# New unit orders, split weights in two steps, a halved down projection and another first root in a fused attention and FFN kernel

## What is computed

```python
x = L0_attn_x                                  # (4, 512, 256), fp32
xn = _layernorm(x, axis=-1)
s = _L0_attn_ref(xn, Wq, Wk, Wv, Wo)           # 16 heads of 16, causal softmax
g = _silu(_L0_ffn_ref(xn, wq_gate, s_gate, wq_up, s_up, wq_down, s_down))
x = x + s * g
```

## Time and profile before

| | us |
|---|---|
| median of 3 runs (285.98 to 288.08) | 287.1 |
| the profiled execution | 287.32 |
| its span | 285.6 |
| TensorE busy in the span | 272.3 |
| VectorE busy | 209.5 |
| ScalarE busy | 174.0 |
| GpSimd busy | 133.1 |

### The profile page before, as it was taken

How to read it: one execution, slowest core, us unless ns; L and a number is a source line. 1 busy time by engine, 2 the same in 40 slices (tenths; PEclk the granted TensorE clock), 3 DMA queues, 4 the chain that set the end, 5 groups by cost and what they waited for, 6 DMA issues and landing times.

```text
span 285.6 us, 5873 instructions
## 1 busy us (share of the span) xinstructions
PE 272.3 (95%) x2088; PEld 202.0 (71%) x2088; DVE 209.5 (73%) x722; ACT 174.0 (61%) x258; POOL 133.1 (47%) x235
## 2 busy tenths in 40 slices
...
GB/s 266 328 165 203 182 5 2 76 3 112 187 220 9 3 0 6 76 182 153 190 6 6 0 2 3 37 42 137 158 158 77 2 3 2 148 3 3 2 2 73
DMA packets 18005, 23.11 MB, mean 81 GB/s; under 512 B 2936, under 2 KB 11064, under 8 KB 17976
## 3 DMA queue, kind: packets, MB, share of 16 engines
...
...
## 4 chain that ended last, share of the span: by engine, by line
PE 73%; DVE 17%; issue 2%; POOL 2%; DMA 2%; SPq 2%; ACT 1%; ACTq 1%; DVEq 0%
PE ps L428 15%; PE ps L430 12%; PE ps L429 12%; PE ps L578 12%; DVE ps L1007 10%; PE ps L561 8%; PE ps L543 6%; PE ps L588 3%; DMA tailt<-in_su 2%; DVE mx L1007 2%; PE ps L597 1%; PE ps L472 1%; DVE cn L1018 1%; POOL kp L809 1%; DVE hid L986 1%
## 5 line engine op out<-in xcount | busy, mean ns | idle before, releaser
L1007 DVE CUSTOM_DVE_ANT_0 ps<-ps,maskt 128x512 f32<-128x512 f32 (+3 forms) x256 | 117.5, 523 | 16.2 <-PE ps L543 15.7
L854 POOL TENSOR_SCALAR_AFFINE_SELECT pt<-pt 128x256 f32<-128x256 f32 (+1 forms) x112 | 47.7, 442 | 88.2 <-ACT pt L781 87.2
L781 ACT ACTIVATE pt<-ps 128x1024 f32<-128x1024 f32 x80 | 79.4, 1025 | 9.9 <-PE ps L561 8.3
L830 POOL TENSOR_TENSOR hid<-hid 128x512 f32<-128x512 f32 x24 | 32.0, 1333 | 18.4 <-DVE hid L986 9.4
L578 PE MATMUL ps<-pt,vt 128*32 128x256 f32 (+3 forms) x528 | 39.2, 439 | 0.3 <-DVE mx L1007 0.2
L428 PE MATMUL ps<-xh,guh 128*128 128x512 f32 x88 | 37.8, 430 | 1.1 <-DVE xr L979 0.4
L1007 DVE DVE_READ_ACCUMULATOR2_ANT mx<- 128x1 f32 x256 | 36.0, 141 | 0.0
L543 PE MATMUL ps<-kp,qp 64*128 64x512 f32 (+3 forms) x256 | 32.9, 342 | 2.0 <-DVE mx L1007 1.8
L430 PE MATMUL ps<-xh,gul 128*128 128x512 f32 x88 | 34.6, 393 | 0.0
L429 PE MATMUL ps<-xl,guh 128*128 128x512 f32 x88 | 34.5, 392 | 0.0
L561 PE MATMUL ps<-qp,kp 64*128 64x512 f32 (+3 forms) x256 | 33.1, 344 | 0.2 <-DVE mx L1007 0.2
(11 more groups left out here) (121 smaller groups left out, 497.5 us busy)
## 6 DMA issues: line engine op xcount, KB each, us to landing
...
```

Source lines behind the costliest of these rows:

```text
L781: nc.scalar.activation(pair(b, s), ps[:, b0:b1 + 1:b1 - b0, :], ACT.Exp, scale=SCALE).then_inc(exp_done, 1)
L830: nc.gpsimd.tensor_tensor(a, a, hid[:, m % 2, 1, :], ALU.mult).then_inc(h_done, 1)
L854: mm = nc.gpsimd.affine_select(out=diag, in_=diag, compare_op=ALU.is_ge, fill=0.0, base=0, pattern=[[0, diag.shape[1]], [1, P]], channel_m ...
L1007: mm = nc.vector.tensor_tensor_reduce(part, part, maskt[:, T - wide:], -1.0, TOP, ALU.add, ALU.min, mg[:, e, a // 2, i:i + 1])
```

## The change

- `WARM` goes from 36 to 26 zero products, and the four `FILL` products go.
- `transpose_x` waits for each tile of `xn` by itself. All `qk` and `gu` units of row 0 use `first_split`: both high weights by `xh`, both high weights by `xl`, then both low weights by `xh`, each with a wait of its own, so low weights are needed last. `qk:0:0` takes bank 2, which nothing held.
- Each down unit is cut in two, `da` and `dn`, of 17 products each.
- The first root: VectorE writes the variance plus epsilon, ScalarE takes its square root (`sq:0:0`), VectorE takes the reciprocal and does one Newton step (`rt:0:0`), 4 instructions.
- All five lists are new. On ScalarE `xhi` comes before `ghi:0:1` and `whi:0:2`. On VectorE the moments of row 1 come before `wds` and `qlo:0:0`, `wdl` after the first maxima. On TensorE nine projections come before `m:0:0` instead of six. In the tail `oa:3:0` comes after `zt:3:3` and `oa:3:1` after `z2:3:1`.
- The set of units is otherwise the same, with the same sizes.

```diff
@@ constants @@
 NEWTON = 3
-WARM = 36
-FILL = 4
+WARM = 26
 TENSOR_ORDER = """
-t:0:0:0 t:0:1:1 qk:0:0:0 qk:0:1:1 qk:0:2:2 gu:0:0:0 gu:0:1:1 qk:0:3:2 m:0:0:01 m:0:1:34 m:0:2:56 gu:0:2:7 gu:0:3:2
-gu:0:4:0 gu:0:5:7 m:0:3:12 m:0:4:34 gu:0:6:0 gu:0:7:1 gu:0:8:2 m:0:5:01 m:0:6:34 c:0:0:5 gu:0:9:6 v:0:0:0 v:0:1:1
-s:0:0:56 s:0:1:23 m:0:7:07 gu:0:10:4 s:0:2:01 m:0:8:56 s:0:3:23 m:0:9:57 s:0:4:01 m:0:10:26 m:0:11:35 m:0:12:01
-m:0:13:47 c:0:1:2 pv:0:0:6 m:0:14:05 m:0:15:23 t:1:0:1 dn:0:0:6 t:1:1:0 dn:0:1:2 c:0:2:7 qk:1:0:0 zt:0:0:1 m:0:16:23
-s:0:5:45 s:0:6:67 qk:1:1:1 m:0:17:02 s:0:7:34 s:0:8:56 qk:1:2:7 s:0:9:23 m:0:18:04 m:0:19:15 qk:1:3:6 s:0:10:23
...
-z2:3:0:0 dn:3:0:7 s:3:15:01 pv:3:2:2 s:3:16:01 s:3:17:34 s:3:18:56 zt:3:2:2 oa:3:0:7 s:3:19:01 dn:3:1:2 pv:3:3:0
-pv:3:4:1 zt:3:3:0 oa:3:1:2 zt:3:4:1 z2:3:1:0 z2:3:2:1 o:3:0 o:3:1
+t:0:0:0 t:0:1:1 qk:0:0:2 qk:0:1:0 gu:0:0:1 qk:0:2:3 gu:0:1:4 gu:0:2:5 qk:0:3:6 gu:0:3:4 gu:0:4:7 m:0:0:05 m:0:1:16
+gu:0:5:2 gu:0:6:0 gu:0:7:3 gu:0:8:2 m:0:2:17 m:0:3:03 gu:0:9:4 gu:0:10:1 t:1:0:5 m:0:4:06 m:0:5:37 v:0:0:4 m:0:6:02
+v:0:1:1 m:0:7:36 m:0:8:47 t:1:1:0 da:0:0:1 c:0:0:2 da:0:1:3 dn:0:0 m:0:9:02 s:0:0:45 s:0:1:67 dn:0:1 s:0:2:45
+m:0:10:02 s:0:3:67 qk:1:0:1 m:0:11:02 s:0:4:45 c:0:1:3 gu:1:0:6 m:0:12:02 m:0:13:17 m:0:14:34 pv:0:0:5 s:0:5:01
+qk:1:1:2 s:0:6:01 s:0:7:34 zt:0:0:5 gu:1:1:6 s:0:8:01 m:0:15:27 m:0:16:34 c:0:2:5 gu:1:2:6 m:0:17:57 s:0:9:01
...
+s:3:14:23 zt:3:1:7 da:3:0:5 c:3:3:6 dn:3:0 pv:3:2:0 s:3:15:12 s:3:16:34 s:3:17:56 z2:3:0:0 da:3:1:7 s:3:18:12
+s:3:19:34 zt:3:2:5 dn:3:1 pv:3:3:0 pv:3:4:1 zt:3:3:0 oa:3:0:2 zt:3:4:1 z2:3:1:0 oa:3:1:3 z2:3:2:1 o:3:0 o:3:1
 SCALAR_ORDER = """
-init:0:0 whi:0:0 whi:0:1 whi:0:2 ghi:0:0 ghi:0:1 xhi:0:0 xhi:0:1 woh:0:0 qhi:0:0 pkah:0:0 pkal:0:0 qhi:0:1 qhi:0:2
-wdh:0:0 tanh:0:0 up:0:0 qhi:0:3 hhi:0:0 tanh:0:1 up:0:1 tanh:0:2 hhi:0:1 up:0:2 tanh:0:3 hhi:0:2 up:0:3 tanh:0:4
-ccp:0:0 hhi:0:3 up:0:4 vcp:0:0 hhi:0:4 vcp:0:1 exp:0:0 exp:0:1 tanh:0:5 exp:0:2 exp:0:3 exp:0:4 up:0:5 xn:1:0 xn:1:1
...
+init:0:0 sq:0:0 whi:0:0 whi:0:1 ghi:0:0 xhi:0:0 xhi:0:1 ghi:0:1 whi:0:2 qhi:0:0 pkah:0:0 qhi:0:1 woh:0:0 qhi:0:2
+tanh:0:0 up:0:0 pkal:0:0 tanh:0:1 qhi:0:3 xn:1:0 up:0:1 hhi:0:0 wdh:0:0 hhi:0:1 xn:1:1 tanh:0:2 up:0:2 tanh:0:3
+up:0:3 xn:1:2 xn:1:3 hhi:0:2 hhi:0:3 tanh:0:4 up:0:4 tanh:0:5 up:0:5 hhi:0:4 vcp:0:0 hhi:0:5 vcp:0:1 xhi:1:0 xhi:1:1
...
 VECTOR_ORDER = """
-init2:0:0 st:0:0 xn:0:0 wlo:0:0 xn:0:1 xn:0:2 xn:0:3 wlo:0:1 wlo:0:2 xlo:0:0 xlo:0:1 glo:0:0 glo:0:1 qlo:0:0 wds:0:0
-qlo:0:1 qlo:0:2 wol:0:0 gate:0:0 wdl:0:0 qlo:0:3 maxa:0:0 maxb:0:0 gate:0:1 maxa:0:1 maxb:0:1 maxa:0:2 gate:0:2
-maxb:0:2 maxa:0:3 maxb:0:3 maxa:0:4 gate:0:3 maxb:0:4 sh:0:0 bn:1:0 maxa:0:5 gate:0:4 maxb:0:5 bn:1:1 bn:1:2 bn:1:3
-mom:1:0 maxa:0:6 maxb:0:6 maxa:0:7 maxb:0:7 maxa:0:8 maxb:0:8 gate:0:5 maxa:0:9 maxb:0:9 sh:0:1 maxa:0:10 maxb:0:10
...
+init2:0:0 st:0:0 rt:0:0 xn:0:0 xn:0:1 xn:0:2 xn:0:3 wlo:0:0 wlo:0:1 xlo:0:0 xlo:0:1 glo:0:0 glo:0:1 bn:1:0 bn:1:1
+bn:1:2 bn:1:3 mom:1:0 wds:0:0 qlo:0:0 gate:0:0 qlo:0:1 qlo:0:2 gate:0:1 qlo:0:3 wol:0:0 maxa:0:0 maxb:0:0 wdl:0:0
+gate:0:2 maxa:0:1 gate:0:3 maxb:0:1 wlo:0:2 maxa:0:2 maxb:0:2 maxa:0:3 maxb:0:3 gate:0:4 maxa:0:4 gate:0:5 maxb:0:4
+maxa:0:5 maxb:0:5 maxa:0:6 hlt:0:0 sh:0:0 maxb:0:6 maxa:0:7 xlo:1:0 maxb:0:7 maxa:0:8 maxb:0:8 bn:2:0 xlo:1:1 bn:2:1
...
 GPSIMD_ORDER = """
-init3:0:0 vones:0:0 sc:0:0 rows:0:3 rows:0:4 rows:0:5 hid:0:0 hlo:0:0 hid:0:1 hlo:0:1 hid:0:2 hlo:0:2 hid:0:3
...
+init3:0:0 rows:0:3 vones:0:0 rows:0:4 rows:0:5 sc:0:0 root:1:0 root:1:1 root:1:2 root:1:3 hid:0:0 hid:0:1 hlo:0:0
...
 SYNC_ORDER = """
-init4:0:0 loadx:1:0 pkh:0:0 pkl:0:0 pkh:0:1 pkh:0:2 pkh:0:3 pkl:0:1 pkl:0:2 pkl:0:3 loadres:0:0 crow:0:0 crow:0:1
-loadx:2:0 crow:0:2 pkh:1:0 pkl:1:0 pkh:1:1 pkl:1:1 pkh:1:2 pkh:1:3 crow:0:3 loadx:3:0 pkl:1:2 pkl:1:3 crow:1:0
...
+init4:0:0 loadx:1:0 pkh:0:0 pkh:0:1 pkh:0:2 pkl:0:0 pkl:0:1 pkh:0:3 pkl:0:2 pkl:0:3 loadres:0:0 loadx:2:0 crow:0:0
+pkh:1:0 crow:0:1 pkl:1:0 loadx:3:0 pkh:1:1 pkl:1:1 crow:0:2 pkh:1:2 pkl:1:2 crow:0:3 pkh:1:3 pkl:1:3 crow:1:0
...
...
                             w.need("gate", gate_done, HT * b + n // 2 + 1)
                         if n % 2 or n == GUN - 1:
                             w.need("up", up_done, HT * b + n // 2 + 1)
-                    elif kind == "dn":
+                    elif kind == "da":
                         w.need("u", u_done, KD * b + n + 1)
                     elif kind == "c":
                         w.need("ct", ct_copied, NG * b + n + 1)
@@ -466,27 +465,31 @@
 
             def transpose_x(b, k):
                 bank, = take(("t", b, k))
-                if k == 0:
-                    w.need("xn", xn_done, TT * (b + 1))
                 for i in range(TT):
+                    w.need("xn", xn_done, TT * b + i + 1)
                     mm = nc.tensor.transpose(ps[:, bank, i * P:(i + 1) * P], xn[:, i, k * P:(k + 1) * P], ident[:])
                 mm.then_inc(xt_ready, 1)
 
+            def first_split(dst, hi, lo, cols, hi_name, hi_sem, lo_name, lo_sem, part):
+
+                w.need(hi_name, hi_sem, part)
+                for k in range(KD):
+                    w.need("xhi", xhi_done, k + 1)
+                    nc.tensor.matmul(dst, hi[:, k, cols], xh[:, k, :], start=k == 0, stop=False)
+                for k in range(KD):
+                    w.need("xlo", xlo_done, k + 1)
+                    nc.tensor.matmul(dst, hi[:, k, cols], xl[:, k, :], start=False, stop=False)
+                w.need(lo_name, lo_sem, part)
+                for k in range(KD):
+                    mm = nc.tensor.matmul(dst, lo[:, k, cols], xh[:, k, :], start=False, stop=k == KD - 1)
+                return mm
+
             def project_qk(b, c):
                 bank, = take(("qk", b, c))
-                w.need("wl", wl_done, 1 if c == 0 else 2)
                 col = c * P
-                if b == 0 and c == 0:
-                    zeros(FILL, bank)
-                    for k in range(KD):
-                        w.need("xhi", xhi_done, k + 1)
-                        nc.tensor.matmul(ps[:, bank, :], wh[:, k, col:col + P], xh[:, k, :], start=k == 0, stop=False)
-                        nc.tensor.matmul(ps[:, bank, :], wl[:, k, col:col + P], xh[:, k, :], start=False, stop=False)
-                    for k in range(KD):
-                        w.need("xlo", xlo_done, k + 1)
-                        mm = nc.tensor.matmul(ps[:, bank, :], wh[:, k, col:col + P], xl[:, k, :], start=False,
-                                              stop=k == KD - 1)
-                    mm.then_inc(qk_ready, 1)
+                if b == 0:
+                    first_split(ps[:, bank, :], wh, wl, slice(col, col + P), "wh", wh_done, "wl", wl_done, min(c, 1) + 1
+                                ).then_inc(qk_ready, 1)
                     return
                 w.need("xlo", xlo_done, KD * (b + 1))
                 for k in range(KD):
...
 
             def gate_up(b, n):
                 bank, = take(("gu", b, n))
-                w.need("xlo", xlo_done, KD * (b + 1))
-                w.need("gul", gul_done, 1 if n % 2 == 0 else 2)
                 at = (n // 2 if n % 2 == 0 else HF + 1 + n // 2) * P
                 cols = slice(at, at + P)
+                if b == 0:
+                    first_split(ps[:, bank, :], guh, gul, cols, "guh", guh_done, "gul", gul_done, n % 2 + 1
+                                ).then_inc(gu_ready, 1)
+                    return
+                w.need("xlo", xlo_done, KD * (b + 1))
                 for k in range(KD):
                     mm = split3(ps[:, bank, :], guh[:, k, cols], gul[:, k, cols],
                                 xh[:, k, :], xl[:, k, :], k == 0, k == KD - 1)
                 mm.then_inc(gu_ready, 1)
 
-            def down(b, n):
-                bank, = take(("dn", b, n))
+            def down_first(b, n):
+                bank, = take(("da", b, n))
                 w.need("hlo", hlo_done, HF * (b + 1))
                 w.need("hlt", hlt_done, b + 1)
                 w.need("wdl", wdl_done, 1)
-                for i in (2 * n, 2 * n + 1):
-                    rows = slice(i * P, (i + 1) * P)
-                    dst = ps[:, bank, (i % 2) * D:(i % 2 + 1) * D]
-                    for m in range(HF):
-                        split3(dst, hh[:, m, rows], hl[:, m, rows], wdh[:, m, :], wdl[:, m, :], m == 0, False)
-                    nc.tensor.matmul(dst, hh[:, HF, rows], wdh[:, HF, :], start=False, stop=False)
-                    mm = nc.tensor.matmul(dst, hh[:, HF, rows], wdl[:, HF, :], start=False, stop=True)
-                mm.then_inc(f_ready, 1)
+                down_tile(2 * n, bank)
+
+            def down_rest(b, n):
+                down_tile(2 * n + 1, bank_of("da", b, n)).then_inc(f_ready, 1)
+
+            def down_tile(i, bank):
+                rows = slice(i * P, (i + 1) * P)
+                dst = ps[:, bank, (i % 2) * D:(i % 2 + 1) * D]
+                for m in range(HF):
```

(37 more changed lines are left out.)

134 lines of the change are left out of this document (59 added, 75 removed).

## The result

| | before | after |
|---|---|---|
| median, us | 287.59 (285.98 to 288.26, 4 runs) | 272.27 (272.11 to 272.46, 4 runs) |
| ratio, 95% interval | | 0.9475 (0.9433 to 0.9518) |
| span of the profiled execution, us | 285.6 | 270.4 |
| mean granted TensorE clock | 0.994 | 0.998 |

The changed kernel is 15.3 us faster. The forecast was 8.85 us, with a range down to 275.0, so the sign was right and the size far off.

A forecast was written before the change was run, and what follows sets the result against it. TensorE bounds the kernel, with VectorE a second bound from 14 to 50 us. Head 3.1, waits 2.0, clock 1.45, changes 2.1, tail 0.5, less 0.3, sum to 8.85: 287.32 becomes 278.5, for the median 278.3; range 275.0 to 284.2.

The forecast's parts named there:

- Head: Up to the first projection: earlier root and xn, no FILL; qk:0:0 ends near 12.65 instead of 15.73, gain 3.1 us.
- Rival B: First 50 us: VectorE bounds them, gains only the root's 1.0 us, waits for row 1; 286 to 287 us, chance 0.07.
- Zero products and FILL: TensorE's warm-up: 20 passes fewer save 2.0 to 2.9 us, so it ends at 9.0 (8.5 to 9.4).
- Rival D: Head: with fewer zero products the clock falls before qk:0:0, nine projections take 12.2 us more; 290.5 us, chance 0.03.
- Tables: ScalarE: a second table load of 1.28 us before tanh:0:0, for the square root, falls into slack; costed at nothing.
- Waits: TensorE's idle: 2.0 of 3.9 us before 50.5 us goes, 2.36 us behind stays; 0.3 us allowed for new waits.
- Changes of kind: TensorE's list: switches between full products, m or s, and pv fall from 142 to 121; 0.1 us each, 2.1 us.
- Clock: TensorE's low-clock stretch behind the early idle pieces goes; a pv unit there took 3.73 against 2.29 us, gain 1.45 us.
- Tail: End of TensorE's list: oa:3:0 moves from ahead of the last pv into a stretch with waits; gain 0.5 of 0.7 us.
- Rival C: Whole kernel, everything works: all 3.9 us idle before 50.5 us goes, switches give 4, tail 0.7; 273.5 us, chance 0.10.

The follow-up runs named there:

- e2: Changed kernel's new lists with the old head code (old root, WARM 36, FILL 4, split3, one wait for all of xn): 273.76 us, ratio 0.9510.
- e1: Kernel before, its old lists kept but for what the new head code needs, with the new head code: 287.86 us, ratio 1.0009.
- e6: e1 with one stretch of ScalarE's list reordered, so no q or k copy stands behind the DMA of woT: 288.44 us, ratio 1.0040.
- e7: Changed kernel with the old root alone (bit trick, three Newton steps on VectorE, no ScalarE square root): 272.21 us, ratio 0.9468.
- e3: Changed kernel with the down projection whole: each da unit runs both halves, dn nothing: 278.43 us, ratio 0.9664.
- e4: Changed kernel with unread TensorE products added at the end, full and narrow, grouped then alternating: 0.18 us a change, 7.3 us for 40.

## Why the prediction was right and wrong

- *Head.* Every station from the root on was right within 0.5 us (root, `xn`, `xh`, first and second projection, `m:0:0`). The 3.1 us measured 2.9 as a position. As a part of the result it was about 1 us (e2), and alone 0 (e1, e6). That the whole 3.1 us would be kept was the step here that did not hold; it is hidden in the total.
- *Rival B* had a chance of 0.07, "the same list end is reached at the same time". In e1 and e6, where the orders were left out, the time came out as it says, but by another way. B has VectorE wait for row 1 of x. There VectorE was early by 2 us at `xlo:0:0` and lost it before 26 us, for the most part idle for ScalarE (1.98 us for `tanh:0:0`, 2.04 us for `wdh`). From then on VectorE was as full as B says, up to 36 us.
- *Zero products and FILL.* The first transpose behind the warm-up started at 9.45 (forecast 9.0, 8.5 to 9.4). With the same 26 products it started at 8.92 in e7 and 8.96 in the repeated changed kernel. `xh` waited for `ghi:0:0`, up to 10.1, so this cost nothing. Rival D, the clock falling in the new head, did not come in the changed kernel. It did come in e1, behind a wait of 1.90 us: not for want of zero products, but for want of ready work.
- *Tables.* Costed at nothing and seen at nothing in the changed kernel. In e1, where the load stands behind `wdh`, `tanh:0:0` started only at 21.35, and VectorE waited 1.98 us for it. So the term is nothing only where ScalarE's list covers the load, as in the changed kernel and in e6 (`tanh:0:0` at 18.30).
- *Waits: the step that failed.* "I take 2.0 of the 3.9 us idle before 50.5 us as gone (0 to 3.5) and leave the 2.36 us behind it." Two faults lie in it. The larger is its second half. The waits behind 50.5 us were left standing with no reason but that I had not gone through them; the new lists took away 3.3 of their 3.6 us. The other is the measure. The idle column was taken for the loss: 6.75 us idle is 10.05 us of late starts in the profile before, since each wait also swallows the overlap of two products. By idle the first half was right (2.1 us gone), by starts it is 2.9. The tail gave 0.8. The halving of the down projection belongs here as well: I priced it at nothing in either direction, and without it, in these lists, 6 us come back (e3).
- *Changes of kind: right mechanism, mis-sized.* I read 0.09 us on the way in and 0.10 on the way back from the earlier trace rows and spread them as 0.1 a change. The third piece is in the same rows: 0.72 us from 82.13 to 82.85 for eight products that take 8 x 0.0735 = 0.59 in a row. By start excess the 21 changes gave 2.9 us (forecast 2.1), by e4's price 3.8.
- *Clock.* As forecast: no low stretch up to 264 us, and the slow `pv` unit of the earlier trace rows is gone. The size was right too. The kernel before took 285.87 and 286.10 us in its runs with a mean clock of 1.000 and about 287.5 in those with 0.994, so one low stretch costs some 1.5 us (forecast 1.45).
- *Tail.* As forecast. From the start of the last `pv` unit to TensorE's last product it is 6.36 us before and 6.45 after, though the six products of `oa:3:0` (0.7 us) now lie in it.
- *Range.* Rival C, where everything works, priced all waits at 3.9 us. With waits by starts, 7 to 9 us, its end would have been near 269. But the range took in only half of C, so by the same rule it would have ended near 273, still a little above 272.3.

What stays open: which of the new lists removes which wait. Whole lists can hardly be exchanged one by one, since each engine's list has to fit the others, so it wasn't tried.
